# A four-stage, one-core kernel: the next sequence's transposes, products and copies moved earlier in the first stage

## The reference, cut to what matters

```python
x = x0                                            # (8, 512, 128), float32
q    = x @ Wq                                     # 8 heads of 16
feat = elu(q) + 1
KV   = sum_s feat_s (x) q_s ;  Ksum = sum_s feat_s
msg  = (feat @ KV) / (feat . Ksum + 1e-6)         # per head
m2   = msg @ Wm
a    = x + layernorm(m2) * g1 + b1
a    = a + layernorm(relu(m2 @ W1) @ W2) * g2 + b2
x1   = plain_layernorm(x + a)                     # = norm(2x + b1 + b2 + gained norms)
logits = x1 @ router_w.T                          # then softmax, top 8 of 64, capacity 64 per expert
```

## Time and profile before

| What | Value |
|---|---|
| Time before, median of 3 runs | 634.9 us (633.05 to 636.92) |
| The profiled execution's own time | 639.89 us |
| Its span in the trace | 637.8 us |
| First stage in it, to the first pick round | 0 to 141.86 us |
| Busy over the span | TensorE 88%, VectorE 73%, GpSimd 68%, ScalarE 48% |

### The profile page before, as it was taken

How to read it: one execution, slowest core, us unless ns; L and a number is a source line. 1 busy time by engine, 2 the same in 40 slices (tenths; PEclk the granted TensorE clock), 3 DMA queues, 4 the chain that set the end, 5 groups by cost and what they waited for, 6 DMA issues and landing times.

```text
span 637.8 us, 10359 instructions
## 1 busy us (share of the span) xinstructions
PE 562.8 (88%) x3195; PEld 460.7 (72%) x3195; DVE 464.8 (73%) x1566; ACT 305.5 (48%) x825; POOL 434.1 (68%) x478
## 2 busy tenths in 40 slices
PE   5988889879557999889998999989999899999993
PEld 4777767754346787667787878878878788787772
DVE  1567877869999544576669778788688787976862
ACT  3547776438611222333636636546456473672440
POOL 6453434316667777648878979979889898653672
PEclk9979998879855555699999999999999999999996
DMA  4696764559821222343020300401204000000000
GB/s 132 167 308 238 273 255 175 208 213 207 172 64 48 59 67 63 136 161 133 20 114 10 120 21 10 141 0 49 103 9 141 1 9 10 10 9 1 10 8 16
DMA packets 47224, 62.03 MB, mean 97 GB/s; under 512 B 13026, under 2 KB 39873, under 8 KB 46146
## 3 DMA queue, kind: packets, MB, share of 16 engines
q1 hardware_dynamic: 44610, 56.15, 27.5%
q0 software_dynamic: 2560, 5.23, 2.9%
HBM read 35.16 MB, written 24.13 MB: 93 GB/s over the span
## 4 chain that ended last, share of the span: by engine, by line
PE 49%; DVE 21%; issue 4%; POOL 4%; DMA 2%; ACT 2%; POOLq 0%; SPq 0%; DVEq 0%
PE pair L1421 8%; PE pair L1423 8%; PE pair L1422 8%; PE pair L1754 4%; DVE cand L1950 3%; DVE keyT L1952 3%; DVE c_g L1222 2%; PE pair L1533 2%; PE pair L1469 2%; PE pair L1543 2%; POOL c_acc L934 2%; PE pair L1764 2%; PE pair L1538 2%; DVE c_x L1193 2%; PE pair L1460 1%
## 5 line engine op out<-in xcount | busy, mean ns | idle before, releaser
L934 POOL TENSOR_TENSOR c_acc<-c_acc,c_g 128x512 f32<-128x512 f32 x112 | 144.7, 1292 | 37.6 <-DVE c_g L1222 30.3
L1070 ACT ACTIVATE c_sg<-pair 128x256 f32<-128x256 f32 x256 | 95.3, 386 | 93.3 <-PE pair L1423 90.7
L1222 DVE SCALAR_TENSOR_TENSOR c_g<-pair,c_comb,c_sg 128x256 f32<-128x256 f32 x224 | 100.3, 477 | 27.3 <-ACT c_sg L1070 23.1
L1421 PE MATMUL pair<-c_w_hi,c_x3h 128*128 128x512 f32 x256 | 109.0, 426 | 12.2 <-DVE c_g L1222 11.3
L1423 PE MATMUL pair<-c_w_hi,c_x3l 128*128 128x512 f32 x256 | 101.0, 395 | 0.0
L1422 PE MATMUL pair<-c_w_lo,c_x3h 128*128 128x512 f32 x256 | 100.7, 393 | 0.0
L1421 PEld LDWEIGHTS pair<-c_w_hi,c_x3h 128*128 128x128 f32 x256 | 48.2, 188 | 23.5 <-DVE c_g L1222 14.1
L1423 PEld LDWEIGHTS pair<-c_w_hi,c_x3l 128*128 128x128 f32 x256 | 48.0, 188 | 11.3
L1422 PEld LDWEIGHTS pair<-c_w_lo,c_x3h 128*128 128x128 f32 x256 | 48.3, 189 | 8.1
L1827 POOL DMA_INDIRECT rows_all<-token_rows,tok_row x32 | 31.3, 978 | 14.8 <-issue 8.8
L1832 POOL DMA_INDIRECT routed_rows<-x1T_all,dest_row x32 | 31.8, 993 | 10.3 <-issue 7.3
(11 more groups left out here) (373 smaller groups left out, 1504.0 us busy)
## 6 DMA issues: line engine op xcount, KB each, us to landing
routed_rows<-rows_all SPq DMA_DIRECT2D x8, 2048.0 KB
c_c<-routed_rows SPq DMA_DIRECT2D x7, 2048.0 KB, 7.8
token_rows<-a_xw SPq DMA_DIRECT2D x8, 384.0 KB, 2.8
a_x<-in_L_attn_x SPq DMA_DIRECT2D x8, 256.0 KB, 3.0
base_all<-a_xw SPq DMA_DIRECT2D x8, 256.0 KB, 3.4
c_c<-routed_rows SPq DMA_DIRECT2D x4, 512.0 KB, 5.2
out<-c_outb SPq DMA_DIRECT2D x16, 128.0 KB, 1.8
wgu_late<-in_L_ffn_w_gate SPq DMA_DIRECT2D x4, 480.0 KB, 7.6
```

Source lines behind the costliest of these rows:

```text
L934: g.tensor_tensor(acc, acc, b["g"][:, (2 * uf + i) % 4, :, :], ALU.add).then_inc(s["acc"], 1)
L1070: a_.activation(b[f"sg{q % 2}"][:, x, :], self.pair[q % 2][:, x, H1:2 * H1], SIG).then_inc(s["sig"], 1)
L1222: v.scalar_tensor_tensor(out=dst, in0=self.pair[q % 2][:, x, 0:H1], scalar=b[f"comb{uf}"][:, j * E1 + e:j * E1 + e + 1], in1=b[f"sg{q % 2} ...
L1421: t.matmul(dst, w_hi, x_hi, start=start, stop=False)
```

## The change

In a pass k whose next sequence is "ahead" (sequences 1 to 6, by `ahead`), TensorE transposes the next x right behind kv, with a wait for featT's copy, and makes its q right behind the numerators; ScalarE copies xT behind the sums of squares of m, and reads q (relu and copy) ahead of x1T's copy; only the exponential comes behind msgT's copy. For sequence 7 the transposes stay where they were and q comes behind msg's transposes. In all passes: the sums of squares of l come before x1 on ScalarE; the logits (L653) come behind msg's transposes, and the copy lg behind msgT's copy and the exponential; the three unread products of each pass are gone. The residual is halved: r = x + (b1 + b2) / 2 in one instruction, with g1 and g2 halved once and the last norm's epsilon divided by 4, so x1 stays the same. The diff, without the edits to setup lines already told:

```diff
@@ pool @@
-                g.tensor_tensor(r3, x3, x3, ALU.add).then_inc(s["r_half"], 1)
-                pool.wait_ge(s["r_half"], n + 1)
-                g.tensor_tensor(r3, r3, bcast_mid(b["b12"][:, 0, :], NT), ALU.add).then_inc(s["r_step"], 1)
+                g.tensor_tensor(r3, x3, bcast_mid(b["b12"][:, 0, :], NT), ALU.add).then_inc(s["r_step"], 1)
@@ act: head of the loop @@
+        def read_q(n):
+            act.wait_ge(s["q_mm"], n + 1)
+            if n:
+                act.wait_ge(s["feat_sb"], n)
+            a.activation(b["e"][:, :], bank[2][:, :], ACT.Relu, scale=-1.0).then_inc(s["negq"], 1)
+            if n:
+                act.wait_ge(s["kv_mm"], n)
+            else:
+                act.wait_ge(s["consts"], self.consts_q)
+            a.copy(b["q"][:, :, 0:D], bank[2][:, :].rearrange("p (j d) -> p j d", d=D)).then_inc(s["q_sb"], 1)
@@ act: behind the sums of squares of m @@
+            if self.ahead(k + 1):
+                copy_xT(k + 1)
             n = k - 3
...
+            n = k - 1
+            if 0 <= n < self.N:
+                act.wait_ge(s["l_mm"], n + 1)
+                act.wait_ge(s["var_m"], n + 1)
+                square_sums("sq", bank[4], NT).then_inc(s["var_l"], 1)
@@ act: behind x1 (L336) @@
-                square_sums("sq", bank[4], NT).then_inc(s["var_l"], 1)
+            if self.ahead(k + 1):
+                read_q(k + 1)
@@ act: end of the pass, behind msgT's copy (L366); lg's copy (L360) now follows these lines @@
+            if k + 1 < self.N:
+                if not self.ahead(k + 1):
+                    read_q(k + 1)
+                exponential(k + 1)
@@ pe @@
+        def q_products(n):
+            pe.wait_ge(s["xT_sb"], n + 1)
+            if not self.ahead(n) and n:
+                pe.wait_ge(s["key_sb"], 1)
+            for j in range(NT):
+                ins = t.matmul(bank[2][:, j * D:(j + 1) * D], b["xT"][:, j * P:(j + 1) * P], b["Wq"][:, :], start=True, stop=True)
+            ins.then_inc(s["q_mm"], 1)
...
                 ins.then_inc(s["kv_mm"], 1)
+                if self.ahead(k + 1):
+                    pe.wait_ge(s["featT_sb"], n + 1)
+                    x_transpose(k + 1)
...
                 ins.then_inc(s["num_mm"], 1)
+                if self.ahead(k + 1):
+                    q_products(k + 1)
...
+                transposes(bank[0], tile("msg")).then_inc(s["msgT_mm"], 1)
+                if k + 1 < self.N and not self.ahead(k + 1):
+                    q_products(k + 1)
@@ pe: the logits (L653) now follow these lines; removed from their old place @@
-                unread(3, bank[0])
-                pe.wait_ge(s["msg_sb"], n + 1)
-                transposes(bank[0], tile("msg")).then_inc(s["msgT_mm"], 1)
```

More of the change, by code:

```diff
@@ L144, in event, with ahead @@
         return i // 2, i % 2
+    def ahead(self, n):
+        return 0 < n < self.N and n - 1 not in self.EVENTS
     def stored(self, eng):
@@ L172, in consts @@
         chain(g.tensor_tensor(b["b12"][:, 0, :], b["b12"][:, 0, :], b["b12"][:, 1, :], ALU.add))
+        chain(g.tensor_scalar(b["b12"][:, 0, :], b["b12"][:, 0, :], 0.5, None, ALU.mult))
         chain(g.memset(b["tri"][:, :], -1.0))
@@ L234, in pool @@
                     pool.wait_ge(s["x1_sb"], n)
[L235 removed]
+                g.tensor_scalar(b["rstd3"][:, :], mv[:, :, 1], EPS / 4, None, ALU.add).then_inc(s["rstd3_step"], 1)
                 g.tensor_scalar(b["nmu"][:, :], mv[:, :, 0], -1.0, None, ALU.mult).then_inc(s["rstd3_step"], 1)
@@ L285, in copy_xT, with exponential @@
             a.copy(b["xT"][:, :], bank[1][:, :]).then_inc(s["xT_sb"], 1)
+        def read_q(n):
[8 more added lines that the diff above has]
+            a.copy(b["q"][:, :, 0:D], bank[2][:, :].rearrange("p (j d) -> p j d", d=D)).then_inc(s["q_sb"], 1)
+        def exponential(n):
+            act.wait_ge(s["negq"], n + 1)
+            a.activation(b["e"][:, :], b["e"][:, :], ACT.Exp, scale=-1.0).then_inc(s["eq"], 1)
         copy_xT(0)
+        read_q(0)
+        exponential(0)
         for k in range(self.N + 3):
[L289 to L303 removed]
+            if k == 0:
+                setup_transposed()
             n = k - 1
@@ L353, in act @@
                 a.copy(self.x1T_all[:, at * L:(at + 1) * L], bank[0][:, :]).then_inc(s["x1T_kept"], 1)
-            if k + 1 < self.N:
+            if k + 1 < self.N and not self.ahead(k + 1):
                 copy_xT(k + 1)
-            if 0 <= n < self.N:
-                act.wait_ge(s["lgt_mm"], n + 1)
-                if n >= 2:
-                    act.wait_ge(s["mask_sb"], n - 1)
-                a.copy(b[f"lg{n % 2}"][:, :], bank[5][:, 0:NT * E0]).then_inc(s["lg_sb"], 1)
             n = k
@@ L366, in act @@
                 a.copy(b["msgT"][:, :], bank[0][:, :]).then_inc(s["msgT_sb"], 1)
+            if k + 1 < self.N:
+                if not self.ahead(k + 1):
+                    read_q(k + 1)
+                exponential(k + 1)
+            n = k - 2
+            if 0 <= n < self.N:
+                act.wait_ge(s["lgt_mm"], n + 1)
+                if n >= 2:
+                    act.wait_ge(s["mask_sb"], n - 1)
+                a.copy(b[f"lg{n % 2}"][:, :], bank[5][:, 0:NT * E0]).then_inc(s["lg_sb"], 1)
     def dve(self, dve):
@@ L378, in setup @@
             v.tensor_scalar(b["Wmc"][:, :], b["Wm"][:, :], b["wmu"][:, 0:1], None, ALU.subtract)
+            for name in ("g1", "g2"):
+                v.tensor_scalar(b[name][:, :], b[name][:, :], 0.5, None, ALU.mult)
             for h in range(2):
@@ L389, in gain @@
                 dve.wait_ge(s["add"], 2 * n)
+            else:
+                dve.wait_ge(s["setup_dve"], 3)
             v.tensor_tensor(b["g" + name][:, :].rearrange("p (j d) -> p j d", d=D), src[:, :].rearrange("p (j d) -> p j d", d=D),
@@ L560, in pe @@
         x_transpose(0)
-        for k in range(self.N + 3):
-            n = k
-            if n < self.N:
-                pe.wait_ge(s["xT_sb"], n + 1)
-                if n == 7:
-                    pe.wait_ge(s["key_sb"], 1)
-                for j in range(NT):
-                    ins = t.matmul(bank[2][:, j * D:(j + 1) * D], b["xT"][:, j * P:(j + 1) * P], b["Wq"][:, :], start=True, stop=True)
-                ins.then_inc(s["q_mm"], 1)
-                if n == 0:
-                    setup_transposes()
+        def q_products(n):
[5 more added lines that the diff above has]
+            ins.then_inc(s["q_mm"], 1)
+        q_products(0)
+        setup_transposes()
+        for k in range(self.N + 3):
             n = k - 1
@@ L628, in pe @@
                 transposes(bank[0], lambda j: b[f"xw{n % 2}"][:, j, 0:D]).then_inc(s["x1T_mm"], 1)
-            if k + 1 < self.N:
-                if k in self.EVENTS:
-                    pe.wait_ge(s["maskT_sb"], 1)
+            if k + 1 < self.N and not self.ahead(k + 1):
+                pe.wait_ge(s["maskT_sb"], 1)
                 x_transpose(k + 1)
@@ L644, in pe @@
                 t.matmul(rank[:, :], b["tri_r"][:, :], b["maskT"][:, h, :], start=False, stop=True).then_inc(s["rank_mm"], 1)
+            n = k
+            if n < self.N:
+                if n >= 2:
+                    pe.wait_ge(s["x1T_kept"], n - 1)
+                pe.wait_ge(s["msg_sb"], n + 1)
+                transposes(bank[0], tile("msg")).then_inc(s["msgT_mm"], 1)
+                if k + 1 < self.N and not self.ahead(k + 1):
+                    q_products(k + 1)
+            n = k - 2
             if 0 <= n < self.N:
```

26 lines of the change are left out of this document (1 added, 25 removed).

## The result

The changed kernel took 640.99 us in the median of 22 runs (634.95 to 643.04), the kernel before 635.98 in as many (632.75 to 640.38). The ratio is 1.0061, 95% interval 1.0044 to 1.0078: slower by 0.6%, about 3.9 us. The forecast was 634.3 in a range of 630.0 to 639.5. The profiled execution after took 641.08 us, its span is 639.2.

What follows compares the result with a forecast made beforehand. It took the loop last norm, x1, sums, gain, message, feat to bound the first stage, 13.07 us a pass. Terms -1.0 - 0.5 - 1.4 - 1.0 + 3.3 = -0.6 us on 634.9 gave 634.3, range 630.0 to 639.5.

Steps and rivals of the forecast that it cites:

- The new wait of W1 for lg's copy: Each pass: W1 products start 2.27 us behind the message instead of 1.44, a wait of 0.83 us.
- the middle pass: Loop of a middle pass at full clock: 12.81 us against 13.07, a gain of 0.26 a pass.
- x's landing: Load of x for pass 3, queued behind the zeros: lands at 51.3 us, though needed at 48.4.
- the residual priced at nothing: VectorE's first adds lose about 0.75 us of waiting for GpSimd; no gain in middle passes, as TensorE is busy anyway.
- pass 3: Message at 57.9 us against 58.93 after the wait for x: -1.0 us.
- passes 6 and 7: Event passes, sequence 7 not ahead: last W1 29.65 us behind the message of pass 5, against 31.1: -1.4 us.
- passes 4 and 5: Two middle passes, each gaining 0.26 us: -0.5 us.
- pass 8: x1 no longer stands ahead of the sums of l on ScalarE: -1.0 us.
- The clock term: TensorE's thinner work in the first stage makes its granted clock fall more often: +3.3 us, bounds 0 to 13.4.
- Two falls' worth more than before: Of the new thin stretches on TensorE, two more clock falls at 1.65 us each: 3.3 us.
- The clock makes it slower: Rival, 26 in 100: TensorE's clock falls in nearly every pass; 639.2 us from the fifth fall, 641 with two long.
- The clock stays up: Rival, 27 in 100: TensorE's clock doesn't fall; -3.9 us, 631.0, or 628.1 if x lands in time too.

Runs made afterwards that it cites:

- The old order at full clock: The kernel before with each 2 MB write of zeros issued one pass later; ratio 1.0023, its profile's clock up until 127.9 us.
- The cut kernels: Six kernels without everything after the last keys, output a copy of the base rows; means: before 155.0 us, changed 158.5 us.
- A third pair: The changed kernel with x's transposes behind the W2 products and zeros one pass later, without and with two unread products; full-kernel ratios 0.9985 and 0.9990.

## Why the prediction was wrong

**What held.** The new wait of W1 for lg's copy (2.34 against 2.27), the middle pass (12.92 against 12.81), the gain of pass 2 (39.07 against 38.8), the W1 products behind the message of pass 2, x's landing (51.63 against 51.35), the residual priced at nothing, and W1 of pass 7 at 105.07 - 100.31 = 4.76 behind the message (17.0 - 12.4 = 4.6 forecast). The last W1 came 29.93 behind the message of pass 5 at full clock, in the variant with x's transposes late, forecast 29.65.

**The step that failed: the base of the sum at full clock.** The forecast compared moments of the changed kernel at full clock with moments of the old kernel that had its own falls in them. It took the message of pass 3 at 58.93 and the last W1 at M5 + 31.1 as the old kernel's; the first has the fall at 40.2 in it, the second those at 98.2 and 111.8. It had itself noted that passes 6 and 7 hold the old kernel's own falls. The old order at full clock shows 56.98 and 28.07. With the forecast's own moment for pass 3, where no run of the changed kernel kept its clock, and with measured ones behind it:

- pass 3: 57.9 - 56.98 = +0.9, where it said -1.0;
- passes 4 and 5: 2 x (12.92 - 13.06) = -0.3, where it said -0.5;
- passes 6 and 7: 29.93 - 28.07 = +1.9, where it said -1.4 (by its own 29.65, +1.6);
- pass 8: 13.93 - 15.28 = -1.4, where it said -1.0.

That is +1.1 at full clock and not -3.9. The cut kernels put it at 0.7, with 2 either way. So neither shows a gain in the order of work: what the middle passes and pass 8 win, the wait for x and pass 7 lose. In pass 7 the message-to-W1 stretch went from 97.93 - 96.16 = 1.77 us to 4.76, since q's products, which need the key, and q's three steps on ScalarE stand ahead of lg there. The forecast had this 4.6 in its working and hid it behind the inflated 31.1.

**The clock term** was 3.3 us, and 2.8 is the estimate from the runs. That the two are close is partly luck: the forecast took 6.6 us more at half speed at half price, and the cut kernels showed 9.9 at a price of 0.28. The mechanism, thinner work of TensorE, more time at half speed, is shown by taking the unread products out of the old kernel (117.1 to 125.6 us on one chip, and 0.5% slower); putting them into the changed one brought 126.1 down to 117.7, across two groups of runs. A third pair, in the variant, showed it only across two chips (25.9 and 17.1) and not on one (137.1 and 135.4). The term was added to a sum that had already counted the old kernel's falls as gains. "Two falls' worth more than before" is only right beside a base from which the falls of before have been taken out. With both put right, 1.1 + 2.8 = 3.9 us, the measured loss, closer than the uncertainty of either term. The rest of the distance from 634.3 to 640.99 is the base of the time: the forecast stood on a median of 634.9 from 3 runs, and 22 runs gave 635.98.

**Its rivals.** *The clock makes it slower* came true in its sign and near its number (639.2 forecast, 636.0 + 3.9 measured), but not in its mechanism: it asked for five falls' worth, 8.2 us, and there were 2.8; of the missing 5.4 us, 5.0 are the base's (-3.9 to +1.1). *The clock stays up* fell with the stretch at 50.9. The trace also disagrees with the rule weighed there from the Trainium skill, page "TensorE: Matmul & The Clock Gate" (section "Why this matters for your kernels"), that long idle gaps are what matters: in the kernel after, the clock fell at 88.5 with no idle time of TensorE over 0.95 us in the two passes ahead of it, and an idle time of 1.52 us instead of 0.70 a pass went with 8.5 us more at half speed in the old order.

**What stays open.** The variant that is best in the first stage alone (x late, zeros later, two unread) is 3.3 us faster there and only 0.7 in the full kernel (654 us x 0.001; by the interval 2.2 faster to 0.9 slower), though its full runs show as much time at half speed as the kernel before (135.4 and 135.4). If it has 6.5 us less in the first stage, it has as much more behind it, which at 0.28 would be 1.8 of the missing 2.6 us. That is an inference from two groups of runs on different chips, not shown. Also open is why the sums moved ahead of x1 alone raised the half-speed time by 9 us, and what pass 3 of the changed kernel takes at full clock: its profile has a fall there.

## What to carry to other kernels

Before you subtract moments of two kernels, check the granted clock of every stretch that lies before them: a base read from a profile with falls makes a forecast at full clock look like a gain (here by 5 us). When an edit moves work ahead, price the passes that are exempt from it (here the one before an event) on their own, since the exempt order is new too. When an instruction leaves the loop, look at what then stands ahead of the next link: the sums moved ahead of x1 alone shortened the pass by 0.05 us. Filler products belong into a gap that another engine's work sets, not ahead of an instruction on the path; the same three cost 0.6 us a pass in one place and nothing in the other, and two in a gap that the middle passes have cost 0.8 us over the passes that don't have it.

## What the runs showed of the hardware

Removing 0.89 us of products that nobody reads from each of eight passes made the kernel 0.5% slower. By the fit, one microsecond at half speed cost about 0.28 us, not 0.5, in the first stage; in single stretches 0.26 and 0.44. The load of x, 256 KB, issued right behind the issue of 2 MB of zeros by the same engine, landed 8.5 us later, where before the change, issued 2.7 us after their issue had ended, it took 5.8, and with no zeros ahead of it, in the kernel before with later zeros, 2.6. And the placing of the half-speed stretches changes from run to run so much that the first picks of two kernels that the runs don't tell apart (before, and before with later zeros) lay at 141.9 and 137.6 us in their profiles.
